# Another order of the attention step, with one weight piece per step

## The chip, the cores and the metric

The kernel runs on one core of a Trainium2 chip. The metric is the device time of one execution in microseconds. One core has five engines that run side by side and meet only at semaphores: TensorE (PE in the profile, its weight loads PEld), VectorE (DVE), ScalarE (ACT), GpSimd (POOL) and SyncE (SP), which here issues DMAs alone.

## The reference

32 samples are turned into rows of 256 numbers: 1 class row, 36 image patches and 77 text tokens, the text after four recurrent layers. On these 114 rows per sample follows one attention block and one mixture of experts. Cut to what the change touches:

```python
n = layernorm(h)
qk = silu(n @ wqk + bqk);  q = qk * gamma[0] + beta[0];  k = qk * gamma[1] + beta[1]
v = silu(n @ wv + bv)
attn = where(causal, laplacian(q @ k.T / S + bias), 0)
h = h + attn @ v
x = layernorm(h)
logits = x @ w_router.T            # 8 experts, the best 2 of each row, softmax over both
h = h + layernorm(sum of the two experts' outputs, weighted) * gain + bias
```

## The kernel before

The text layers run first, up to about 550 us of the span, then the attention stage, then 64 blocks of 128 sorted rows through the experts (from 715 us), and the final sums.

The attention stage works on 8 groups of 4 samples. Each engine has a function `attn_step(g)` (ACT line 958, POOL line 1182, PE line 1504, DVE line 1984) that is called for g = 0 to 10, unrolled. The order of the calls in it is the order of the engine's instructions, and engines take their instructions strictly in that order. In step g the attention of group g is computed, the attended sums of group g-1 are added, the normalized rows of group g-2 are turned and routed, and the rows of group g-3 get their places and are sent. In detail:

- ACT: `query_key_silu`, `query` and `key` make q and k of group g. `norm_rows(g+1)` and `rows_turned(g+1)` normalize the next group and copy its transposes from PSUM (banks 0 and 1). `gate_values(g, half)` makes the values, `score_gelu(g)` the gelu, with a load of the activation table on either side. `routed_norm(g)` (870) normalizes the rows for the router, `routed_turned` (882) copies their transposes (banks 6 and 0), and `weight(g)` (887) waits for DVE's `choose(g)`, which has the gap between the two best logits.
- PE: `query_key`, `values`, `scores`, `attended(g, half)` (1399), `turn_rows` (1374) and `turn_routed` (1411) for the transposes, `router` (1421: 16 products of 8 columns) and `ranks` (1431). `turn_rows(g+1, 0)` writes bank 0, so it waits until both parts of `routed_turned(g-2)` are done. `query_key(g)` needs both parts of `rows_turned(g)`.
- DVE: `scale_scores`, `invert` (1900, a reciprocal), `weigh`, `add_attended`, the statistics of both norms, `choose` (1934) and `count` (1946) for the best experts, `place_rows` (1965).
- POOL: the inverse roots of the norms, and `send_rows` (1166), 8 indirect DMAs for each group, 64 in all, that scatter the rows into `xrows` in DRAM. The first expert block is loaded when all have landed.
- SP: lines 667 to 671 load the gate and up weights in 8 pieces of 1 MB, two at a time: the next two are issued when the former two have landed (`ld_ffn`) and enough groups are added (`a_h2`). The first two have neither wait; they stand behind the loads of `h_all`.

Six of the pieces have to be split into an upper part (ACT, `upper_weights(k)`, line 826, waits for `ld_ffn` to show pieces 2*(k//2) and 2*(k//2)+1) and a lower part (DVE, `lower_weights(k)`, line 1869, waits for the upper one). Before, three are split in the tail of the attention stage (ACT in step 8, DVE in step 10) and three after it.

Of the kernel before, what the change touches and what calls it, by code (L numbers as in the profile page):

```python
# [22 lines left out]
GROUPS = BATCH // GB  # L23
# [145 lines left out]
def has(g):  # L169

    return not isinstance(g, int) or 0 <= g < GROUPS


def build(nc, patches, patches_tail, tokens, tok_w, tok_b, cls, pos_enc, tok_emb, pos_emb, w_in, w_b, w_c, w_out,
          small, ln_gb, wqk, wv, bv, rel_bias, w_gate, w_up, w_down, ffn_gb, consts, out):
    ctx = ExitStack()
    with ctx:
# [158 lines left out]
        assert at[0] <= 3 * FC * GT  # L336

        EMBEDDED = 5
        SPLIT_FIRST = 3
        BIAS_OPS = 3 * 3 + 11  # L340
        LAST_LAG = 3
        SENT_FIRST = 5
# [377 lines left out]
        def _(act):  # L720
# [105 lines left out]
            def upper_weights(k):  # L826
                act.wait_ge(ld_ffn, 32 * (k // 2 + 1))
                hi, _, raw = FFN_HALVES[k]
                act.activation(hi, raw, ACT.Copy).then_inc(w_upper, 1)

            def norm_rows(g):
                act.wait_ge(a_bias, g + 1)
                wait(act, a_tr, g * 2)
                for b in range(GB):
                    norm = act.activation(a_n[:, b, :], h_all[:, g * GB + b, :], ACT.Identity, bias=a_nb[:, b:b + 1],
                                          scale=a_rs[:, 0, b:b + 1])
                norm.then_inc(a_norm, 1)
# [6 lines left out]
            def query_key_silu(g):  # L844
                act.wait_ge(a_qkm, g + 1)
                wait(act, a_qkd, g)
                act.activation(a_qk, bank[2][:, 0:GS], ACT.Silu, bias=SML(W_QK)).then_inc(a_qks, 1)

            def query(g):
                act.wait_ge(a_qks, g + 1)  # L850
                wait(act, a_sm, g)
                act.activation(a_q, a_qk, ACT.Identity, bias=SML(W_QK + 3), scale=SML(W_QK + 1))

            def key(g):
                act.activation(a_k, a_qk, ACT.Identity, bias=SML(W_QK + 4), scale=SML(W_QK + 2)).then_inc(a_qkd, 1)

            def score_gelu(g):
                act.activation(warm[:, 0:1], minus_half[0:1, 0:1], ACT.Gelu)
                act.wait_ge(a_sa, g + 1)
                wait(act, a_om, g * 2)  # L860
                act.activation(a_w, a_arg, ACT.Gelu).then_inc(a_er, 1)
                act.activation(warm[:, 1:2], minus_half[0:1, 0:1], ACT.Silu)

            def gate_values(g, half):
                act.wait_ge(a_vm, g * 2 + (half + 1))
                wait(act, a_om, g * 2 - 1 + half)
                act.activation(a_v[:, 2 * half:2 * half + 2, :],
                               bank[3][0:SEQ, :].rearrange("p (k d) -> p k d", k=2), ACT.Silu).then_inc(a_vs, 1)

            def routed_norm(g):  # L870
                act.wait_ge(m_bias, g + 1)
                if g == 0:
                    for half in range(2):
                        act.wait_ge(seq_stored[2 + half], 16 * len(rows_out[half]) * GROUPS // 2)
                wait(act, m_tr, (g - ROW_SETS) * 2 + 2)
                wait(act, x_sent[g % ROW_SETS], g // ROW_SETS * (16 * 2 * GB))
                for b in range(GB):
                    norm = act.activation(a_x[g % ROW_SETS][:, b, 0:D], h_all[:, g * GB + b, :], ACT.Identity,
                                          bias=m_nb[:, b:b + 1], scale=m_rs[:, 0, b:b + 1])
                norm.then_inc(m_norm, 1)  # L880
# [77 lines left out]
            def attn_step(g):  # L958
                if has(g) and g:
                    query_key_silu(g)  # L960
                if has(g - 2):
                    routed_turned(g - 2, 0)
                    routed_turned(g - 2, 1)
                if has(g):
                    query(g)
                    key(g)
                if has(g + 1):
                    norm_rows(g + 1)
                if has(g - 2):
                    weight(g - 2)  # L970
                if has(g):
                    gate_values(g, 0)
                    score_gelu(g)
                if has(g + 1):
                    rows_turned(g + 1, 0)
                    rows_turned(g + 1, 1)
                if has(g):
                    gate_values(g, 1)
                if g - 1 == GROUPS - 1:
                    for k in range(SPLIT_FIRST):  # L980
                        upper_weights(k)
                if has(g - 1):
                    routed_norm(g - 1)

            for g in range(GROUPS + LAST_LAG):
                attn_step(g)


            for k in range(SPLIT_FIRST, len(FFN_HALVES)):
                upper_weights(k)  # L990

            def turn(j, k):
                act.wait_ge(f_tr, j + 1)
# [233 lines left out]
        def _(pe):  # L1227
# [276 lines left out]
            def attn_step(g):  # L1504
                if has(g) and g:
                    query_key(g)
                if has(g - 2):
                    turn_routed(g - 2, 0)
                    turn_routed(g - 2, 1)
                if has(g - 3):  # L1510
                    ranks(g - 3)
                if has(g):
                    values(g, 0)
                if has(g - 2):
                    router(g - 2)
                if has(g):
                    scores(g)
                if has(g - 1):
                    attended(g - 1, 0)
                    attended(g - 1, 1)  # L1520
                if has(g + 1):
                    turn_rows(g + 1, 0)
                    turn_rows(g + 1, 1)
                if has(g):
                    values(g, 1)
                if has(g + 1):
                    bias_scores(g + 1)

# [77 lines left out]
        def _(dve):  # L1606
# [377 lines left out]
            def attn_step(g):  # L1984
                if has(g - 3):
                    place_rows(g - 3)
                if has(g + 1) and g:
                    norm_bias(g + 1)
                if has(g + 2):
                    norm_ahead_stats(g + 2)  # L1990
                if g - 2 == GROUPS - 1:
                    for k in range(SPLIT_FIRST):
                        lower_weights(k)
                if has(g - 2):
                    choose(g - 2)
                if has(g):
                    scale_scores(g)
                if has(g - 1):
                    add_attended(g - 1, 0)
                    add_attended(g - 1, 1)  # L2000
                    routed_stats(g - 1)
                if has(g - 2):
                    count(g - 2)
                if has(g - 1):
                    routed_bias(g - 1)
                if has(g):
                    invert(g)
                    weigh(g)

            for g in range(GROUPS + LAST_LAG):  # L2010
                attn_step(g)
# [34 lines left out]
            dve.tensor_copy(expert_i[:, :], expert_f).then_inc(tbl_ready, 1)  # L2046
            c.done()
            dve.wait_ge(tbl_ready, 2)
            for k in range(SPLIT_FIRST, len(FFN_HALVES)):
                lower_weights(k)  # L2050


            def hidden(j, k):
# [151 lines left out]
```

## Time and profile before

| what | us |
|---|---|
| median of 3 runs | 1121.9 (1121.77, 1121.9, 1126.06) |
| profiled execution, its own time | 1125.7 |
| its span | 1123.9 |
| text layers, until about | 550 |
| attention stage, first gelu to last `slot_i` | 554.9 to 692.4 |
| last row sent to first expert product | 708.7 to 716.7 |
| PE busy | 975.9 (87%) |
| DVE, ACT, POOL busy | 758.9, 601.9, 577.5 |

The span goes from the first to the last instruction; the execution's own time has 1.8 us around it. The attention stage has eleven steps, of which eight bear the whole attention of a group.

### The profile page before, as it was taken

The numbers are of one execution on the slowest core, as the hardware profiler recorded it, in microseconds if no ns is written. First come the engines' busy times: TensorE is split into PE (matmuls) and PEld (weight loads), VectorE is DVE, ScalarE is ACT, GpSimd is POOL, SyncE is SP. The second block draws the span as 40 slices with busy tenths as digits, with TensorE's granted clock in tenths as the row PEclk, the third lists the DMA queues.
The fourth block names the chain that finished last, engine by engine and source line by source line (L and its number), as shares of the span: only waits on it lengthen the run. The fifth ranks groups of instructions, "written<-read, shape, count | busy, mean of one in ns | idle before, by whom it ended". The sixth has DMA issues, their size and how long they took to land.

```text
span 1123.9 us, 20592 instructions
## 1 busy us (share of the span) xinstructions
PE 975.9 (87%) x5838; PEld 846.4 (75%) x5839; DVE 758.9 (68%) x1966; ACT 601.9 (54%) x1343; POOL 577.5 (51%) x630
## 2 busy tenths in 40 slices
PE   5878999999999999999898962499999999999910
PEld 4668999999999999998666652377777777777710
DVE  1666999999999998998678767244444444444447
ACT  1466776877788777666697753123223223223223
POOL 4523765567667766777627767232222222222236
PEclk8998999999999999999999975699999999999965
DMA  9451001000100000012168236133233333333263
GB/s 278 130 151 57 1 1 66 1 2 1 67 1 2 1 25 2 10 58 57 36 212 260 61 76 224 52 47 50 47 47 49 49 47 47 47 50 48 43 162 118
DMA packets 54733, 75.49 MB, mean 67 GB/s; under 512 B 9348, under 2 KB 46978, under 8 KB 52612
## 3 DMA queue, kind: packets, MB, share of 16 engines
q1 hardware_dynamic: 32680, 49.24, 14.5%
q0 software_dynamic: 16640, 18.53, 10.1%
q10 hardware_dynamic: 5340, 6.83, 2.2%
q8 instruction: 36, 0.59, 0.2%
q14 instruction: 37, 0.30, 0.1%
HBM read 45.38 MB, written 29.14 MB: 66 GB/s over the span
## 4 chain that ended last, share of the span: by engine, by line
PE 68%; DVE 10%; POOL 7%; DMA 5%; issue 4%; ACT 3%; SPq 2%; POOLq 0%; ACTq 0%; DVEq 0%
PE bank L1264 16%; PE bank L1580 10%; PE bank L1329 7%; PE bank L1557 6%; PE bank L1566 5%; PE bank L1565 4%; PE bank L1324 3%; POOL xrows L1174 3%; PE bank L1560 3%; PE bank L1572 2%; DMA xtok<-in_tok_emb,tokens_s 2%; PE bank L1312 2%; SPq L541 1%; POOL xtok L1052 1%; DVE arena_b L1736 1%
## 5 line engine op out<-in xcount | busy, mean ns | idle before, releaser
L1203 POOL DMA_INDIRECT yrows<-arena_b,dest_i x64 | 99.2, 1550 | 268.2 <-ACT arena_b L1009 260.3
L1736 DVE SCALAR_TENSOR_TENSOR arena_b<-bank,sml,arena_b 128x304 f32<-128x304 f32 (+2 forms) x384 | 195.3, 522 | 20.7 <-ACT arena_b L778 17.9
L1264 PE MATMUL bank<-xt_hi,w_hi 128*128 128x308 f32 x512 | 159.9, 312 | 4.6 <-DVE arena_b L1736 3.2
L1264 PE MATMUL bank<-xt_hi,w_lo 128*128 128x308 f32 x512 | 157.3, 307 | 0.0
L1264 PE MATMUL bank<-xt_lo,w_hi 128*128 128x308 f32 x512 | 156.9, 306 | 0.0
L2057 DVE TENSOR_TENSOR arena_b<-bank,arena_b 128x512 f32<-128x512 f32 x64 | 44.3, 691 | 140.5 <-PE bank L1566 76.7
L1090 POOL TENSOR_TENSOR u_halves<-arena_b,u_halves 128x308 fp32r<-128x308 f32 x128 | 109.8, 865 | 29.8 <-ACT arena_b L790 29.7
L1084 POOL TENSOR_TENSOR y_lo<-arena_b,y_hi 128x308 fp32r<-128x308 f32 x128 | 107.9, 857 | 27.2 <-ACT y_hi L802 27.0
L1264 PEld LDWEIGHTS bank<-xt_hi,w_hi 128*128 128x128 f32 x512 | 98.0, 191 | 5.4 <-DVE arena_b L1736 3.5
L1580 PE MATMUL bank<-arena_b 128*128 x384 | 98.7, 393 | 1.2 <-DVE arena_b L2073 0.9
L1264 PEld LDWEIGHTS bank<-xt_hi,w_lo 128*128 128x128 f32 x512 | 98.0, 191 | 0.0
L1264 PEld LDWEIGHTS bank<-xt_lo,w_hi 128*128 128x128 f32 x512 | 97.8, 191 | 0.0
L1174 POOL DMA_INDIRECT xrows<-arena_b,slot_i x64 | 77.7, 1214 | 33.7 <-issue 16.9
L778 ACT ACTIVATE arena_b<-bank,sml 128x308 f32<-128x308 f32 x128 | 77.0, 602 | 17.4 <-PE bank L1264 12.0
L1002 ACT ACTIVATE arena_b<-bank 128x512 f32<-128x512 f32 x64 | 38.4, 599 | 85.5 <-PE bank L1560 85.5
L2073 DVE COPY arena_b<-bank 128x512 f32<-128x512 f32 x64 | 44.3, 691 | 56.6 <-PE bank L1572 56.6
L1329 PE MATMUL bank<-w_hi,y_hi 128*128 128x256 f32 (+1 forms) x320 | 82.1, 283 | 0.0
L1329 PE MATMUL bank<-w_lo,y_hi 128*128 128x256 f32 (+1 forms) x320 | 81.6, 282 | 0.0
L1744 DVE SCALAR_TENSOR_TENSOR bank<-arena_b,sml,bank 128x308 f32<-128x308 f32 x128 | 68.1, 534 | 19.5 <-PE bank L1313 19.3
L1009 ACT ACTIVATE arena_b<-bank,row_wt 128x256 f32<-128x256 f32 x64 | 30.4, 475 | 93.5 <-PE bank L1580 93.5
L1580 PEld LDWEIGHTS bank<-arena_b 128*128 128x128 f32 x384 | 67.8, 189 | 16.0 <-issue 5.9
L995 ACT ACTIVATE x_hi<-bank 128x256 fp32r<-128x256 f32 x64 | 24.6, 384 | 95.9 <-PE bank L1547 95.9
(212 smaller groups left out, 2650.3 us busy)
## 6 DMA issues: line engine op xcount, KB each, us to landing
arena_b<-xrows SPq DMA_DIRECT2D x64, 129.5 KB, 2.1
wg_raw<-in_w_gate SPq DMA_DIRECT2D x4, 1024.0 KB, 7.1
yrows<-arena_b SPq DMA_DIRECT2D x1, 3648.0 KB, 18.7
h_all<-seq SPq DMA_DIRECT2D x8, 448.0 KB
w_raw<-in_w_in SPq DMA_DIRECT2D x3, 1024.0 KB, 4.8
arena_b<-in_w_down SPq DMA_DIRECT2D x3, 1024.0 KB, 8.6
wu_raw<-in_w_up SPq DMA_DIRECT2D x2, 1024.0 KB, 7.3
wu_s<-in_w_up SPq DMA_DIRECT2D x2, 1024.0 KB, 9.4
```

Of the source, the lines that this page charges most:

```text
L778: act.activation(u[s % 2][:, c, :], x_bank(c)[:, 0:GT], ACT.Identity, bias=SML(W_CB + s // GROUPS * FC + c), scale=conv_w(s // GROUPS, c, ...
L1084: pool.tensor_tensor(y_half(y_lo, s, c), y_full[:, c, :], y_half(y_hi, s, c).bitcast(F32), ALU.subtract)\
L1090: pool.tensor_tensor(u_halves[s % 2][:, 1, c, :], u[s % 2][:, c, :], u_halves[s % 2][:, 0, c, :].bitcast(F32), ALU.subtract).then_inc(pool ...
L1174: pool.indirect_dma_start(xrows, bass.IndirectOffsetOnAxis(ap=to, axis=0), a_x[g % ROW_SETS][:, b, :], None).then_inc(x_sent[g % ROW_SETS] ...
L1203: pool.indirect_dma_start(yrows, bass.IndirectOffsetOnAxis(ap=dest_i[:, m:m + 1], axis=0), f_y[m % 2], None, compute_op=ALU.add).then_inc( ...
L1264: mm = pe.matmul(out_, in_half(w, layer, d, slice(c * P, (c + 1) * P)), x[:, d, cols], start=(k == 0), stop=(k == len(pairs) - 1))
L1329: return pe.matmul(out_tile(j), y[:, c, PAIR_AT[j]:PAIR_AT[j] + PAIR_ROWS[j]], out_half(w, s // GROUPS, c), start=False, stop=stop, skip_g ...
L1557: pe.matmul(bank[0][:, :], x_hi[:, k, d, :], w[:, d, cols], start=(d == 0 and w is wg_hi), stop=False)
L1566: pe.matmul(bank[1][:, :], x_raw[k], wu_s[:, cols], start=False, stop=True).then_inc(f_um, 1)
L1580: mm = pe.matmul(bank[4 + k][:, 0:D], f_ht[k][:, c, :], wd_s[c][:, bass.ds(e * D, D)], start=(c == 0), stop=(c == FC - 1))
L1736: dve.scalar_tensor_tensor(acc[:, :, back_:TXT], x[:, :, 0:TXT - back_], conv_w(s // GROUPS, c, tap), acc[:, :, back_:TXT], ALU.mult, ALU. ...
L1744: dve.scalar_tensor_tensor(y1, u[s % 2][:, c, :], SML(W_D + s // GROUPS * FC + c), y1, ALU.mult, ALU.add)\
```

## The change

ACT: `routed_norm` moves from the end of a step to its beginning and one step later (group g-2 in step g), `routed_turned` behind it into mid-step, `score_gelu` from mid-step to near the end; `weight` now stands ahead of `rows_turned`. PE: `turn_routed` moves from the head of the step behind the first half of `attended`, `turn_rows` ahead of `router`, and the halves of `attended` stand around `router` and `values(g, 1)`. DVE: `choose` and `count` stand together behind `invert`, between the two halves of `add_attended`. The split of the weights is spread: `upper_weights(0)` to `(5)` stand in ACT's steps 2 to 7, `lower_weights(0)` to `(5)` in DVE's steps 3 to 8. The programs of POOL and SP stay as they are.

```diff
--- before.py
+++ after.py
@@ -336,7 +336,7 @@
         assert at[0] <= 3 * FC * GT
 
         EMBEDDED = 5
-        SPLIT_FIRST = 3
+        SPLIT_FROM = 2
         BIAS_OPS = 3 * 3 + 11
         LAST_LAG = 3
         SENT_FIRST = 5
@@ -958,36 +958,32 @@
             def attn_step(g):
                 if has(g) and g:
                     query_key_silu(g)
+                if has(g):
+                    query(g)
+                    key(g)
+                if has(g - 2):
+                    routed_norm(g - 2)
+                if has(g + 1):
+                    norm_rows(g + 1)
+                if 0 <= g - SPLIT_FROM < len(FFN_HALVES):
+                    upper_weights(g - SPLIT_FROM)
                 if has(g - 2):
                     routed_turned(g - 2, 0)
                     routed_turned(g - 2, 1)
                 if has(g):
-                    query(g)
-                    key(g)
-                if has(g + 1):
-                    norm_rows(g + 1)
+                    gate_values(g, 0)
                 if has(g - 2):
                     weight(g - 2)
-                if has(g):
-                    gate_values(g, 0)
-                    score_gelu(g)
                 if has(g + 1):
                     rows_turned(g + 1, 0)
                     rows_turned(g + 1, 1)
                 if has(g):
+                    score_gelu(g)
                     gate_values(g, 1)
-                if g - 1 == GROUPS - 1:
-                    for k in range(SPLIT_FIRST):
-                        upper_weights(k)
-                if has(g - 1):
-                    routed_norm(g - 1)
 
             for g in range(GROUPS + LAST_LAG):
                 attn_step(g)
 
-
-            for k in range(SPLIT_FIRST, len(FFN_HALVES)):
-                upper_weights(k)
 
             def turn(j, k):
                 act.wait_ge(f_tr, j + 1)
@@ -1504,25 +1500,25 @@
             def attn_step(g):
                 if has(g) and g:
                     query_key(g)
-                if has(g - 2):
-                    turn_routed(g - 2, 0)
-                    turn_routed(g - 2, 1)
                 if has(g - 3):
                     ranks(g - 3)
                 if has(g):
                     values(g, 0)
+                    scores(g)
+                if has(g - 1):
+                    attended(g - 1, 0)
+                if has(g - 2):
+                    turn_routed(g - 2, 0)
+                    turn_routed(g - 2, 1)
+                if has(g + 1):
+                    turn_rows(g + 1, 0)
+                    turn_rows(g + 1, 1)
                 if has(g - 2):
                     router(g - 2)
                 if has(g):
-                    scores(g)
+                    values(g, 1)
                 if has(g - 1):
-                    attended(g - 1, 0)
                     attended(g - 1, 1)
-                if has(g + 1):
-                    turn_rows(g + 1, 0)
-                    turn_rows(g + 1, 1)
-                if has(g):
-                    values(g, 1)
                 if has(g + 1):
                     bias_scores(g + 1)
 
@@ -1988,24 +1984,24 @@
                     norm_bias(g + 1)
                 if has(g + 2):
                     norm_ahead_stats(g + 2)
-                if g - 2 == GROUPS - 1:
-                    for k in range(SPLIT_FIRST):
-                        lower_weights(k)
-                if has(g - 2):
-                    choose(g - 2)
+                if 0 <= g - 1 - SPLIT_FROM < len(FFN_HALVES):
+                    lower_weights(g - 1 - SPLIT_FROM)
                 if has(g):
                     scale_scores(g)
                 if has(g - 1):
                     add_attended(g - 1, 0)
+                if has(g):
+                    invert(g)
+                if has(g - 2):
+                    choose(g - 2)
+                    count(g - 2)
+                if has(g - 1):
                     add_attended(g - 1, 1)
                     routed_stats(g - 1)
-                if has(g - 2):
-                    count(g - 2)
+                if has(g):
+                    weigh(g)
                 if has(g - 1):
                     routed_bias(g - 1)
-                if has(g):
-                    invert(g)
-                    weigh(g)
 
             for g in range(GROUPS + LAST_LAG):
                 attn_step(g)
@@ -2046,8 +2042,6 @@
             dve.tensor_copy(expert_i[:, :], expert_f).then_inc(tbl_ready, 1)
             c.done()
             dve.wait_ge(tbl_ready, 2)
-            for k in range(SPLIT_FIRST, len(FFN_HALVES)):
-                lower_weights(k)
 
 
             def hidden(j, k):
```

## Rows read from the trace of the kernel before

**Rows 1.** Timeline of ACT, steps 3 and 7: start us, us, engine, line, what [idle before]
```profile
585.39 0.62 ACT L847 ACTIVATE arena_b<-bank,sml 128x456 f32<-128x456 f32 x1
586.18 0.99 ACT L885 ACTIVATE arena_a<-bank 128x456 f32<-128x456 f32 x2 [0.17 <-PE bank L1417]
587.06 0.77 ACT L852 ACTIVATE arena_b<-arena_b,sml 128x456 f32<-128x456 f32 x1
...
588.38 2.06 ACT L835 ACTIVATE arena_b<-h_all,a_nb,a_rs 114x256 f32<-114x256 f32 x4
591.98 0.21 ACT L890 ACTIVATE arena_b<-arena_b 114x4 f32<-114x4 f32 x1 [1.53 <-DVE arena_b L1944]
592.55 0.60 ACT L867 ACTIVATE arena_b<-bank 114x512 f32<-114x512 f32 x1 [0.36 <-PE bank L1407]
593.16 1.28 ACT L858 ACT_TABLE_LOAD   x1
...
596.56 0.96 ACT L842 ACTIVATE arena_b<-bank 128x456 f32<-128x456 f32 x2
...
598.78 2.08 ACT L878 ACTIVATE arena_b<-h_all,arena_a,arena_b 114x256 f32<-114x256 f32 x4 [0.77 <-DVE arena_a L1930]
...
646.63 0.62 ACT L847 ACTIVATE arena_b<-bank,sml 128x456 f32<-128x456 f32 x1
```

**Rows 2.** Timeline of POOL: first send, a send beside DVE's split, last send
```profile
588.87 1.24 POOL L1174 DMA_INDIRECT xrows<-arena_b,slot_i  x1 [6.06 <-DVE slot_i L1981]
...
681.95 2.27 POOL L1174 DMA_INDIRECT xrows<-arena_b,slot_i  x1 [2.39 <-DVE slot_i L1981]
...
708.65 1.11 POOL L1174 DMA_INDIRECT xrows<-arena_b,slot_i  x1 [0.30 <-issue]
```

**Rows 3.** Timeline of PE, end of the sends to the first expert block
```profile
715.40 0.66 PE L1547 MATMUL bank<-cst,arena_b 128*128 128x128 f32 x2 [22.32 <-DMA arena_b<-xrows]
```

**Rows 4.** Timeline of PE, step 3, at the full clock
```profile
587.21 1.98 PE L1395 MATMUL bank<-arena_a,arena_b 128*114 128x256 f32 x8
589.03 1.67 PE L1427 MATMUL bank<-sml,arena_a 128*114 128x8 f32 x16
...
591.42 1.89 PE L1407 MATMUL bank<-arena_b 114*114 114x256 f32 x8
593.15 0.94 PE L1380 MATMUL bank<-cst,arena_b 114*128 114x114 f32 x8
...
597.57 1.80 PE L1387 MATMUL bank<-arena_b,arena_a 128*128 128x456 f32 x4 [0.73 <-ACT arena_b L842]
```

**Rows 5.** Issues of line 671 on SP: duration ns min/median/max, first and last start us
```profile
L671 SPq DMA_DIRECT2D wg_raw<-in_w_gate x4: 327/398/433, 574.4 to 584.8; - x4
```

**Rows 6.** Waits on SP's queue, 540 to 720 us: us in total, times, longest
```profile
SPq L670 <- DMA wg_raw<-in_w_gate: 15.5, 2, 9.1
```

**Rows 7.** Timelines of ACT and DVE: three pieces of weights each
```profile
669.07 5.50 ACT L829 ACTIVATE wg_hi<-wg_raw 128x2048 fp32r<-128x2048 f32 x3
...
680.94 6.68 DVE L1872 TENSOR_TENSOR wg_lo<-wg_raw,wg_hi 128x2048 fp32r<-128x2048 f32 x3
```

**Rows 8.** Timeline of PE where the clock is low
```profile
616.13 1.00 PE L1417 MATMUL bank<-cst,arena_b 114*128 114x114 f32 x8 [1.39 <-ACT arena_b L878]
...
617.81 3.37 PE L1395 MATMUL bank<-arena_a,arena_b 128*114 128x256 f32 x8
...
660.90 1.78 PE L1417 MATMUL bank<-cst,arena_b 114*128 114x114 f32 x8 [4.02 <-ACT arena_b L878]
...
664.46 3.23 PE L1427 MATMUL bank<-sml,arena_a 128*114 128x8 f32 x16 [1.15 <-DVE slot_i L1981]
```

**Rows 9.** Stretches: us, busy us of PE, PEld, DVE, ACT, POOL, then PEclk
```profile
600.00:602.00 2.00, 1.10 (x12) 1.10 (x12) 1.90 (x2) 1.82 (x5) 1.40 (x2) 1.00 0.68 148
...
619.00:620.00 1.00, 1.00 (x4) 0.78 (x3) 1.00 (x5) 1.00 (x4) 0.59 (x1) 0.50 0.27 85
...
667.00:668.00 1.00, 1.00 (x5) 0.98 (x6) 0.24 (x2) 0.00 (x0) 0.79 (x1) 0.50 0.34 98
```

## The prediction

> **What bounds the kernel now.** I looked first at the chain of work that ended last, from 560 to 760 us, to see which engine carries the attention stage. It changes hands: ACT and PE in steps 0 to 2 and 5 to 8, POOL's indirect sends in steps 3 to 5 and from 681.95 us to the end. Then the timeline of each engine. ACT's step 3 goes from 585.39 to 600.76, and steps 3 to 6 take (646.63 - 585.39) / 4 = 15.3 us on average [rows 1]. In it ACT stands still in three places only: 1.53 us for the choice of the experts ahead of `weight`, 0.36 for `attended`, 0.77 for the bias ahead of `routed_norm`. The reader is to see how full the step is: nothing can be added to ACT without making it longer, unless a wait shrinks. POOL issues 64 sends from 588.87 to 708.65, of 1.11 us with 0.30 between them [rows 2]; 63 of these make 89 of the 120 us, and most of the rest are norms and waits, so POOL is the next bound, not far behind. The stage ends with POOL's last send, 6.75 us before the first transposes of the expert blocks at 715.40 [rows 2, 3]. The expert blocks themselves are not touched, nor are the text layers; all of the difference must come out between 555 and 715 us.
>
> **The early steps.** In steps 0 and 1 the gelu moves behind `rows_turned`, so `query_key` of the next group need not wait for two table loads. That saves some 3 us by the time of step 2, by my estimate. It is worth nothing, because of the next part.
>
> **The first weight piece.** ACT reaches `upper_weights(0)` in step 2, after q and k (0.62 + 1.32 = 1.94) and two norms of 2.0 each [rows 1], so some 6 us into the step. Step 2 begins at 571 at the latest (585.39 less a step of about 14), so that is 577 at the latest and 574 with the early gain. It waits there for both of the first pieces. SP issues these from 574.4 on, behind the loads of `h_all`, which nothing here moves; and the next two issues stood 9.1 us in the queue for their landing [rows 5, 6]. Two issues of 0.4 and 9.1 us put the landing at 584.3. ACT therefore stands still for 7 to 10 us, and behind it stand `routed_turned(0)`, `gate_values(2, 0)`, the gelu, and by them `turn_rows(3)`, the router and everything that PE has left in the step. From 584.3: the piece 1.83 (5.50 / 3) [rows 7], `routed_turned` 0.88 (586.18 to 587.06) [rows 1], so 587.0. PE has then had no product for some 13 us, and after 4.02 us without one its clock was at 0.50, where 8 transposes took 1.78, the router 3.23 and `values` 3.37 [rows 8, 9]. So: `turn_rows` 1.8, router 3.2, `values` 3.4, `attended` 1.9 (half of 1.89 at twice the time [rows 4]), the bias products about 0.8, `query_key` 1.7, which ends at about 600. Step 3 begins at 600 and not at 585.4: **+14.6 us**. At the full clock it would be 596, or +10.5.
>
> **The steps 3 to 6.** ACT's work in a step: q and k 1.94, two norms 4.0, a piece 1.83, `routed_turned` 0.88, two `gate_values` 1.0, `weight` 0.1, `rows_turned` 0.9, gelu with its tables 3.40 (593.16 to 596.56) [rows 1, 7]: 14.05 us. To this a new wait: `weight` stands ahead of `rows_turned`, and its chain starts only when `routed_turned` is done: `turn_rows` 0.9 (it needs bank 0 free), the router, the choice on DVE. From the router's start (589.03) to `weight` (591.98) is 2.95 us [rows 1, 4]. Of 3.85 us, `gate_values` covers 0.5, so ACT idles 3.35 us in each step where it idled 1.53. Before, `values`, q, k and `norm_rows` lay beside this chain; now nothing does. A step is **17.4 us** at the full clock, and 15.6 even without the piece. DVE (its piece 2.23 [rows 7], ahead of `scale_scores`) and POOL (8 sends, 11.3, and its norms) have room in 17.4; what is late next on DVE is `place_rows`, which waits out the routed norm's bias, but no step hangs on it. The other queue past which something moves is SP's: its third pair of pieces waits for the sums of group 1, which come at about 593 to 598 instead of 580; the pieces are needed two steps later.
>
> **The clock** decides between 17.4 and more. From `scores` to the router's end PE has in each step some 8 us in which it does 32 short transposes and products and nothing at all for about 3.2 us, between `turn_routed` and `turn_rows`. The rows have three gaps to compare: after 4.02 us the clock was 0.50, and stayed there through a router and two `attended`; in a step with a gap of 1.39 us followed by transposes it was 0.50 from 618 to 621; around a gap of 1.54 us that followed the dense `query_key` it stayed at 1.00 at 600 to 602 [rows 8, 9]. A gap of 3.2 with transposes on both sides is nearest to the first two. With the low clock (1.2 in place of 2.4 GHz) `turn_rows` costs 0.9 more and the router 1.6 more, 19.9 us by ACT. But then PE is later than ACT: 8.65 to the end of `routed_turned`, 1.8, 3.2, `values` 3.4, `attended` 0.9 to 1.9, the sum on DVE that frees bank 2 about 0.9, `query_key` 1.7: 20.6 to 21.6, and a little less if the clock is back during `values`. I take 20.8: **+5.5 us a step**, over four steps **+22**. The bounds are 17.4 (+8.4) and 21.6 (+25).
>
> The Trainium skill ("TensorE: Matmul & The Clock Gate", Part 1) says that an idle array falls to 1.2 GHz and only sustained activity lifts it, which speaks against this order. By that rule the forecast stands; by the gap of 1.54 us alone, which the clock survived, it would be 14 us lower.
>
> **The tail.** From step 7 (646.63) to 715.40 are 68.8 us [rows 1, 3]. The three lower pieces, 6.68 us [rows 7], no longer stand on DVE ahead of the last choice, nor do they and the later three lengthen sends (2.27 beside them, 1.24 without [rows 2, 7]). In their place one upper piece stands in step 7 and one lower in step 8, 4.1 us, about half hidden by waits of the routed norm. Between -6.7 and -2.6 I take **-5**. The clock in the tail was low already [rows 9].
>
> **The sum**: 14.6 + 22 - 5 = +31.6 us on the profiled execution's own 1125.7, so 1157.3. The profiled execution was 3.8 us above the median of the runs, so the median is forecast at 1153.5, and I say **1153**. From the bounds: 10.5 + 8.4 - 6.7 = +12 and 14.6 + 25 - 2.6 = +37; this case's own range is 1143 to 1160.
>
> **The rivals.**
> *The clock holds in steps 3 to 6.* The steps are 17.4 us: +14.6 + 8.4 - 7 (a little more, as step 7 is fast too) = +16, 1138. For it: 600 to 602 us. Against: the length of the gap, and what lies around it. Chance 0.24.
> *The first pieces don't stall ACT*, since they land sooner than in this trace or ACT comes later. Then step 3 starts near 586, and the steps cost +8 to +22, less 5: 1125 to 1140, say 1132. Nothing in the rows speaks for it but that the second pair, waiting 15.5 - 9.1 = 6.4 us, landed faster [rows 6]; 2.7 us sooner would still stall. Chance 0.05.
> *POOL sets the end and the order of the others is hidden* (the other side, not slower). Place: the 64 sends. They need 63 x 1.41 = 89 us and about 17 of norms and lengthened sends, 106, where 119.8 passed [rows 2]. If POOL never waited, its first send some 10 us later than 588.87 would still end the stage 3 to 4 us sooner: 1118. It decides from where ACT's step falls to 14.4 us, that is its wait for the choice to 0.35 us. The count of 3.35 says it doesn't. Chance 0.04.
> *The change does less than it says*: the new waits are as long as the old ones and only the tail gains. 1117 to 1125. Chance 0.02.
> The forecast has 0.65.
>
> **How the numbers follow.** The range must leave out at most 2 in 10. It takes in the forecast's case with its upper end, where the low clock also slows `values` and `scores` of the next step (three more us in each step, 1166), and the held clock with a few us below it: 1133 to 1167. About 0.5% (5.6 us) is what a measurement of this kernel can tell from no change. Slower by more: 0.65 + 0.24 + 0.04 of the stall's case = 0.93. Faster 0.03, same 0.04.
>
> **What would show it.** In the changed kernel's timeline of ACT: an idle time of 7 to 10 us ahead of the first upper piece, which starts at about 584.3; steps 3 to 6 of 20 to 21 us between the starts of `query_key_silu`; an idle time ahead of each `weight` of 3.4 us or, with the low clock, near 6, put down to the choice on DVE. On PE, gaps of about 3 us ahead of `turn_rows`, then a router near 3.2, and a granted clock of 0.50 there. No split of weights on DVE after the last choice; the last send at about 740. The forecast is wrong if the first upper piece starts before 580, if the steps are under 16 us, or if the clock stays at 1.00 from 600 to 680.

## The result, and the profile after

The changed kernel takes **1163.0 us** (median of 6 runs, 1157.4 to 1166.5) against 1123.9 for the kernel before in the same runs (6, 1121.4 to 1127.0): 1.0345 times as long, 95% interval 1.0312 to 1.0378, so 39 us slower. Forecast were 1153 and a range of 1133 to 1167. The profiled execution took 1164.9 (span 1163.0), which is 39.2 above that of the kernel before; the sums below are made on these two.

The top of the page of the changed kernel: busy time and share of each engine, then the granted clock in 40 slices.

```profile
PE 996.2 (86%) x5838; PEld 861.6 (74%) x5839; DVE 758.6 (65%) x1966; ACT 601.5 (52%) x1343; POOL 583.5 (50%) x630
...
PEclk8899999999999999999977885599999999999965
```

The counts are those of before (5838, 1966, 1343, 630), and so is the busy time of DVE and ACT within half a microsecond: the same work in another order. PE is busy 20.3 us longer with the same products, because the clock is at 7 to 8 tenths in slices 21 to 24, where it was at 9 before. The other 19 us are idle time of PE.

The timeline of ACT in the changed kernel, steps 2 and 3 with the start of step 4 (start us, us, engine, line, what, then in brackets the idle time ahead and what ended it), for [rows 1]. Line 829 is `upper_weights`, 885 `routed_turned`, 890 `weight`, 842 `rows_turned`:

```profile
572.14 0.62 ACT L847 ACTIVATE arena_b<-bank,sml 128x456 f32<-128x456 f32 x1
...
582.94 1.91 ACT L829 ACTIVATE wg_hi<-wg_raw 128x2048 fp32r<-128x2048 f32 x1 [4.79 <-DMA wg_raw<-in_w_gate]
...
599.91 0.62 ACT L847 ACTIVATE arena_b<-bank,sml 128x456 f32<-128x456 f32 x1
...
605.83 1.89 ACT L829 ACTIVATE wg_hi<-wg_raw 128x2048 fp32r<-128x2048 f32 x1
607.62 0.96 ACT L885 ACTIVATE arena_a<-bank 128x456 f32<-128x456 f32 x2
608.48 0.58 ACT L867 ACTIVATE arena_b<-bank 114x512 f32<-114x512 f32 x1
613.48 0.21 ACT L890 ACTIVATE arena_b<-arena_b 114x4 f32<-114x4 f32 x1 [4.41 <-DVE arena_b L1940]
616.68 0.99 ACT L842 ACTIVATE arena_b<-bank 128x456 f32<-128x456 f32 x2 [2.99 <-PE bank L1391]
617.69 1.28 ACT L858 ACT_TABLE_LOAD   x1
...
621.56 0.61 ACT L847 ACTIVATE arena_b<-bank,sml 128x456 f32<-128x456 f32 x1
```

Line 847 is `query_key_silu`, the start of a step. Steps 1 to 7 start at 559.75, 572.14, 599.91, 621.56, 644.31, 665.99 and 688.79, and PE's first transposes of the expert blocks stand at 754.45. In the kernel before they started at 559.75, 571.23, 585.39, 600.76, 615.99, 632.14 and 646.63, and the transposes at 715.40. So the 39.05 us come in three places:

| | before | after | difference | forecast |
|---|---|---|---|---|
| start of step 3 | 585.39 | 599.91 | +14.5 | +14.6 |
| steps 3 to 6 | 61.24 | 88.88 | +27.6 | +22 |
| step 7 to the expert blocks | 68.77 | 65.66 | -3.1 | -5 |

PE in the changed kernel, its transposes of step 2 and then step 3, for [rows 4, 8]. A row without brackets had no idle time ahead of it:

```profile
585.87 1.75 PE L1376 MATMUL bank<-cst,arena_b 114*128 114x114 f32 x8 [8.63 <-ACT arena_a L885]
...
608.73 0.97 PE L1376 MATMUL bank<-cst,arena_b 114*128 114x114 f32 x8 [3.72 <-ACT arena_a L885]
609.54 2.66 PE L1423 MATMUL bank<-sml,arena_a 128*114 128x8 f32 x16
...
612.83 3.76 PE L1391 MATMUL bank<-arena_a,arena_b 128*114 128x256 f32 x8
...
618.52 1.77 PE L1383 MATMUL bank<-arena_b,arena_a 128*128 128x456 f32 x4 [0.46 <-DVE h_all L1909]
```

Line 1376 is `turn_rows`, 1423 the router, 1391 `values`, 1383 `query_key`. The gap of 3.72 us stands ahead of `turn_rows`, and soon behind it the clock falls: the router takes 2.66 and not 1.67, `values` 3.76 and not 1.98. The stretches of the changed kernel give the clock (us, then busy us of PE, PEld, DVE, ACT and POOL with their counts, PEclk, DMA share, GB/s), for [rows 9]:

```profile
599.90:621.60 21.70, 16.38 (x76) 12.44 (x76) 14.43 (x55) 14.20 (x26) 10.46 (x10) 0.84 0.39 136
621.60:644.30 22.70, 18.06 (x76) 13.93 (x76) 14.71 (x55) 14.09 (x25) 13.29 (x13) 0.77 0.48 147
...
611.00:616.00 5.00, 5.00 (x16) 3.77 (x16) 2.56 (x23) 0.21 (x1) 1.40 (x3) 0.50 0.10 30
```

From 611 to 616 the clock is at 0.50, which is 1.2 GHz in place of 2.4, and PE is busy for all of it. ACT works 14.2 us of 21.7 in a step, as counted (14.05). The rest is the two waits in ACT's rows above, 4.41 and 2.99 us, and the second of them, ahead of `rows_turned` (line 842), stood in no sum.

POOL sends from 602.82 to 747.08 and in each of these steps stands idle for 4.6 to 8.9 us at a time, so it bounds nothing in steps 3 to 6. [rows 2] has its last send 6.75 us ahead of the expert blocks; here it starts at 747.08, 7.37 us ahead of them (the prediction had it at about 740).

### The profile page after: what moved, and what is told of

The parts are those of the page before. It is cut to its first block and busy times, and to the rows that moved or that the text cites. A ratio compares the mean times of both kernels' runs of the same rounds, so it can differ in the third digit from the quotient of the medians.

```text
span 1163.0 us, 20591 instructions
## 1 busy us (share of the span) xinstructions
PE 996.2 (86%) x5838; PEld 861.6 (74%) x5839; DVE 758.6 (65%) x1966; ACT 601.5 (52%) x1343; POOL 583.5 (50%) x630
## 5 line engine op out<-in xcount | busy, mean ns | idle before, releaser
L1170 POOL DMA_INDIRECT xrows<-arena_b,slot_i x64 | 82.2, 1284 | 20.8 <-issue 16.6
L1576 PEld LDWEIGHTS bank<-arena_b 128*128 128x128 f32 x384 | 67.8, 189 | 15.8 <-issue 6.0
```

Source lines behind the costliest of these rows:

```text
L1170: pool.indirect_dma_start(xrows, bass.IndirectOffsetOnAxis(ap=to, axis=0), a_x[g % ROW_SETS][:, b, :], None).then_inc(x_sent[g % ROW_SETS] ...
L1576: mm = pe.matmul(bank[4 + k][:, 0:D], f_ht[k][:, c, :], wd_s[c][:, bass.ds(e * D, D)], start=(c == 0), stop=(c == FC - 1))
```

## The experiments

All are compared with the kernel before, which took 1124.6 to 1125.3 us in these runs. A step is always from one `query_key_silu` to the next.

Two accounts of the later steps are tested. **The choice** is the prediction's: the first piece stalls ACT, the chain through the choice of the experts lengthens each step, the low clock more so, and `rows_turned` is held by the `weight` ahead of it. **The buffer** came from the fence above. `rows_turned(g)` waits for `a_vm` at 2g, which is the end of `values(g - 1, 1)`, since both share the buffer `a_nt`. The change put the router, which has to wait for `routed_turned`, directly ahead of `values(g, 1)`, and moved `rows_turned` ahead of the gelu. ACT's chain is then turned rows, router, `values`, `rows_turned`, gelu, `query_key_silu`, whatever `weight` does.

The expectations have letters. In the first five runs A is the prediction's three causes (stall, longer chain, low clock), B the pieces' own work and C the waits without the clock. In the three runs from the second buffer on, A is the buffer and D the choice. In the last two A is a gain where a piece fills a wait, and E no gain.

### The first piece one step later

```diff
-        SPLIT_FROM = 2
+        SPLIT_FROM = 3
```

> The changed kernel with every weight piece one step later (upper ones in steps 3 to 8, lower ones in steps 4 to 9). Theory A, three causes that add up (the wait for the first pieces in step 2, the longer chain of the new order, the low clock in it): the wait of 4.8 us before the first piece and the cold restart behind it go, step 3 begins near 589 and not at 599.9, steps 3 to 6 keep their 22.2 us, and the time is some 9 us less, about 1154. Rival B, the pieces' own work on ACT and DVE is what costs: there is as much of it as before, so 1163 within 2 us.

Measured: 1155.5 us, 1.0254 (1.0223 to 1.0286), near the 1154 expected. ACT's step 2 goes from 570.68 to 591.73, 21.05 us, against 27.77 in the changed kernel and 14.16 before. So of the 13.6 us that step 2 grew, the piece and its restart are 6.7, and 6.9 would be there without: a step of the new order at the low clock with no piece in it (the granted clock of that step is 0.76). The steps 3 to 6 stay long, at 21.7 on average. The pieces' own work (rival B, 1163) is not what costs the 39 us.

### The order alone, and the pieces alone

The order with the pieces where they were (three at the end of step 8, three behind the stage); and the kernel before with one piece a step:

```diff
# the order alone, ACT (DVE in the same way)
-                if 0 <= g - SPLIT_FROM < len(FFN_HALVES):
-                    upper_weights(g - SPLIT_FROM)
...
+                if g - 1 == GROUPS - 1:
+                    for k in range(SPLIT_FIRST):
+                        upper_weights(k)
...
# the pieces alone, ACT (DVE in the same way)
                     norm_rows(g + 1)
+                if 0 <= g - SPLIT_FROM < len(FFN_HALVES):
+                    upper_weights(g - SPLIT_FROM)
                 if has(g - 2):
                     weight(g - 2)
...
```

> The changed order of the attention step alone, with the weight pieces in the tail as in the kernel before. Theory A: step 3 begins near 588; the gap on PE ahead of turn_rows shrinks to about 2 us; if the clock still falls the steps are near 20.4 us and the time is 1146 to 1150, if it holds they are near 16.5 and the time is about 1132. Rival B: without the pieces in the steps the time is back at 1124 to 1128.

> The order of the kernel before with one weight piece per step from step 2. Theory A: the wait for the first pieces costs some 8 us in step 2, the steps after it stay between 15.0 and 15.8 us since a piece of 1.8 us takes the place of the 1.5 us wait for the choice, and the tail is some 5 us shorter: 1126 to 1131. Rival B: most of the 39 us comes with the pieces, over 1150.

Measured: the order alone 1144.6 us, 1.0159 (1.0120 to 1.0197); the pieces alone 1133.6, 1.0075 (1.0053 to 1.0098). Neither 1132 nor the other branch of the first expectation came quite true, and the pieces cost a little more than expected. From 1124.9 the parts cost 19.7 and 8.8 us, 28.5 together; the change costs 39. Some 10 us arise only when both are there. In the profiles they stand in steps 3 to 6: there the order alone costs 8.9 us, the pieces alone 4.0 and the change 27.6. Order alone, ACT in step 4:

```profile
619.51 0.99 ACT L885 ACTIVATE arena_a<-bank 128x456 f32<-128x456 f32 x2 [0.29 <-PE bank L1417]
620.38 0.61 ACT L867 ACTIVATE arena_b<-bank 114x512 f32<-114x512 f32 x1
624.40 0.21 ACT L890 ACTIVATE arena_b<-arena_b 114x4 f32<-114x4 f32 x1 [3.41 <-DVE arena_b L1944]
625.55 0.99 ACT L842 ACTIVATE arena_b<-bank 128x456 f32<-128x456 f32 x2 [0.93 <-PE bank L1395]
```

And PE in that step, with the stretch of it:

```profile
618.92 0.94 PE L1417 MATMUL bank<-cst,arena_b 114*128 114x114 f32 x8
620.64 0.97 PE L1380 MATMUL bank<-cst,arena_b 114*128 114x114 f32 x8 [0.78 <-ACT arena_a L885]
...
613.20:630.40 17.20, 14.69 (x76) 11.46 (x76) 12.84 (x54) 12.47 (x24) 11.82 (x13) 0.90 0.66 187
```

Here the wait for the choice is 3.41 us, which the prediction had at 3.35, and `rows_turned` waits for `values` even so (0.93). Steps 4 to 6 are 17.2. Without the piece ACT reaches `routed_turned` sooner, so PE's gap ahead of `turn_rows` is 0.78 and not 3.72, and the router behind it runs at the full clock. Most of the 10 us should come from this: the piece stands ahead of `routed_turned`, and so in PE's gap, and the next experiment prices the low clock. But the order alone isn't free of the low clock either. Its step 2 takes 21.0 us at 0.76, with a gap of 1.92, and its step 3, with the same gap, 18.5.

In the pieces alone, ACT waits 8.10 us for the first piece in step 2, which takes 23.7 in place of 14.2. Its steps 3 to 5 are 16.7 to 16.8 each, where I had 15.8 or less. ACT waits 1.6 us for the bias of the routed norm, where it waited 0.77 in step 3 before; DVE's piece of 2.26 us stands ahead of that bias, but no run parts it from the rest. By step 7 both losses stand at 13.5 us, and the tail gives 3.5 of them back.

### The gap filled

To part the clock from the chain: products of constants into an unread part of bank 7, in the gap ahead of `turn_rows`. Twelve of them, then eight, which is about what the gap holds. The wait keeps them off bank 7 until the slots of group g-3 have been read. Nothing is left out of the computation.

```diff
+                if has(g - 2) and has(g + 1):
+                    wait(pe, m_slot, g - 2)
+                    for k in range(FILLERS):
+                        pe.matmul(bank[7][:, 256:512], ident, cst[:, 0:256], start=True, stop=True)
                 if has(g + 1):
                     turn_rows(g + 1, 0)
```

> The changed kernel with 12 products of 256 columns into an unread part of bank 7 between turn_routed and turn_rows in each full step, some 2.9 us of the 3.7 us in which PE stands still there. Theory A, the low clock costs 4 us of each step: the granted clock stays at 1.00 in steps 3 to 6, the router takes about 1.6 us and not 2.7 to 3.1, steps of 18 to 18.5 us, and the time is some 16 us less, about 1147. Rival C, the clock only follows from the waits and ACT sets the step: the steps stay over 21 us, 1160 to 1168.

> The changed kernel with 8 filler products in place of 12. The 12 took 5.4 us of PE and put turn_rows off by 1.5 us, though the clock stayed at 1.00. Theory A (the clock costs 3.8 us a step): 3.6 us of products end before routed_turned does, the clock still stays at 1.00, the steps fall from 19.9 to 18.4 us, 1148 to 1152. Rival C (the products only help by their place, 19.9 us is the chain at the full clock): steps stay at 19.9, or return to 22 as the clock falls, 1157 to 1163.

Measured: twelve 1157.0 us, 1.0281 (1.0251 to 1.0312), missed by 10; eight 1150.7, 1.0242 (1.0218 to 1.0267), as expected. PE in step 3 with twelve, with eight, each with a stretch of its steps:

```profile
602.33 5.36 PE L1517 MATMUL bank<-cst 128*128 128x256 f32 x24
607.52 0.95 PE L1377 MATMUL bank<-cst,arena_b 114*128 114x114 f32 x8
608.31 1.67 PE L1424 MATMUL bank<-sml,arena_a 128*114 128x8 f32 x16
...
597.40:617.30 19.90, 18.14 (x100) 14.57 (x100) 14.43 (x55) 14.17 (x26) 10.06 (x10) 1.00 0.40 138
```

```profile
602.47 3.63 PE L1517 MATMUL bank<-cst 128*128 128x256 f32 x16
606.36 0.97 PE L1377 MATMUL bank<-cst,arena_b 114*128 114x114 f32 x8 [0.26 <-ACT arena_a L886]
...
597.50:616.10 18.60, 16.60 (x92) 12.96 (x92) 14.43 (x55) 14.16 (x25) 10.22 (x10) 1.00 0.45 157
616.10:635.90 19.80, 17.98 (x92) 14.29 (x92) 14.76 (x55) 14.23 (x26) 14.01 (x13) 0.91 0.57 164
```

Twelve products take 5.36 us (each is two instructions in the trace, so x24); the gap is 3.72, and they put `turn_rows` off. The clock is 1.00 in each of steps 3 to 6 and a step takes 19.9. With eight (3.63 us) it takes **18.6** in the two steps at 1.00 (3 and 6) and 19.7 in the two at 0.91. The steps of the changed kernel take 22.2 on average. So the low clock costs 22.2 - 18.6 = 3.6 us a step, some 14 over four. The other 3.3 of the 6.9 us by which a step grew are the chain and the piece.

### A second buffer for the turned rows

The test of the buffer. Groups 2, 4 and 6 get their turned rows in a part of `wu_hi` that is still free, so `rows_turned` waits only for the `values` of two groups before. (PE's `query_key` and `values` read through the same `turned_rows(g)`, which the diff doesn't show.)

```diff
-                wait(act, a_vm, g * 2)
-                act.activation(a_nt[:, d, :], bank[d][:, 0:GS], ACT.Copy).then_inc(a_trc, 1)
+                wait(act, a_vm, max(g - 1, min(g, 1)) * 2)
+                act.activation(turned_rows(g)[:, d, :], bank[d][:, 0:GS], ACT.Copy).then_inc(a_trc, 1)
...
```

> The changed kernel with a second buffer for the turned rows (groups 2, 4 and 6), so that rows_turned no longer waits until values(g, 1) has read the first. Theory A (this wait is what the forecast left out): the 3 us of idle time ahead of rows_turned go in steps 1 to 6, ACT then waits for attended(g-1, 1) ahead of the gelu, and the steps come to the 20.8 us of the forecast, some 1.4 us shorter each, 1156 to 1158. Rival D (the wait for the choice ahead of weight is what makes the step): nothing changes, 1162 to 1165.

Measured: 1157.4 us, 1.0305 (1.0280 to 1.0329), as expected. This interval and that of the change (1.0312 to 1.0378) overlap a little, so it is the profile that decides. ACT in step 3, up to step 4:

```profile
613.20 0.21 ACT L894 ACTIVATE arena_b<-arena_b 114x4 f32<-114x4 f32 x1 [5.61 <-DVE arena_b L1944]
613.32 0.97 ACT L846 ACTIVATE wu_hi<-bank 128x456 f32<-128x456 f32 x2
614.30 1.28 ACT L862 ACT_TABLE_LOAD   x1
615.60 0.20 ACT L862 ACTIVATE warm<-minus_half 1x1 f32<-1x1 f32 x1
617.13 0.58 ACT L865 ACTIVATE arena_b<-arena_b 114x456 f32<-114x456 f32 x1 [1.32 <-PE bank L1407]
...
619.71 0.64 ACT L851 ACTIVATE arena_b<-bank,sml 128x456 f32<-128x456 f32 x1
```

`rows_turned` (line 846) follows `weight` at once, and the wait of 2.99 is gone; 1.32 of it comes back ahead of the gelu, for `attended`. Steps 3 to 6 take 82.6 us in place of 88.9, 20.65 each on average. This is the step that the prediction had costed, and it had it at 20.8.

### The weight later, and the values first

If `rows_turned` hangs on `values`, moving `weight` behind the gelu gives nothing by itself (by the account of the choice it would gain, as the step is then free of it); with `values(g, 1)` also ahead of the router the chain gets shorter.

```diff
# both, ACT
-                if has(g - 2):
-                    weight(g - 2)
                 if has(g + 1):
                     rows_turned(g + 1, 0)
                     rows_turned(g + 1, 1)
                 if has(g):
                     score_gelu(g)
+                if has(g - 2):
+                    weight(g - 2)
# the second alone, PE
-                if has(g - 2):
-                    router(g - 2)
                 if has(g):
                     values(g, 1)
+                if has(g - 2):
+                    router(g - 2)
```

> The changed kernel with ACT's weight(g-2) behind score_gelu. Theory A: the 4.4 to 5.5 us of idle time ahead of weight only move to rows_turned, which waits for values(g, 1) anyway; steps stay at 22.2 us, 1161 to 1165. Rival D (the choice ahead of rows_turned holds ACT up, as the forecast counted it): the steps get over 1 us shorter, 1158 or less.

> As the run with weight behind score_gelu, and on PE values(g, 1) ahead of router(g-2). Theory A: ACT's chain loses the router's 2.7 to 3.1 us, but PE's own sum does not change and query_key ends 1.4 us before ACT takes it; so the steps get about 1.4 us shorter, 1156 to 1158. Rival D: as the run before, no more and no less.

Measured: 1160.4 us, 1.0336 (1.0303 to 1.0369), and 1161.2 us, 1.0337 (1.0316 to 1.0358). Neither ratio can be told from that of the change. In the first the two waits have become one. ACT's rows for it in steps 3 and 4, with PE's router of step 4 between them, and in the second run the rows for it and for the next step:

```profile
614.87 0.99 ACT L842 ACTIVATE arena_b<-bank 128x456 f32<-128x456 f32 x2 [8.70 <-PE bank L1392]
...
629.47 1.68 PE L1424 MATMUL bank<-sml,arena_a 128*114 128x8 f32 x16
...
635.25 0.99 ACT L842 ACTIVATE arena_b<-bank 128x456 f32<-128x456 f32 x2 [6.25 <-PE bank L1392]
```

```profile
631.13 0.99 ACT L842 ACTIVATE arena_b<-bank 128x456 f32<-128x456 f32 x2 [4.69 <-PE bank L1392]
...
638.27 0.64 ACT L847 ACTIVATE arena_b<-bank,sml 128x456 f32<-128x456 f32 x1 [2.01 <-PE bank L1384]
```

8.70 us for `values` alone is what 5.51 and 3.00 were together in step 4 of the changed kernel, with `weight` between them: the router takes 3.12 us in both steps. There the choice didn't hold the step, it only named itself first. But the steps did not all stay at 22.2. Steps 3 and 6 take 22.8 and 23.0, steps 4 and 5 only 20.4 and 20.3. In those two the router runs at the full clock (1.68), in the others at the low one (3.12), so the gain is seen only where the clock differs; whether the move of `weight` brought that about is not shown.

With `values` ahead, the wait is 4.69 in step 4 and about 3.06 in the other three, and the step 20.3 on average. But now `query_key` is late: PE waits 2.22 us ahead of it for DVE's sum. DVE works on `choose` and `count` without a pause from the end of the router to that sum (611.90 to 614.62 in step 3), so here the choice does hold the step, by way of PE. In steps 5 and 6 `query_key` also runs at the low clock (3.38 us against 1.77). The tail is 2.0 us longer than in the changed kernel (67.6). The steps gave what the account of the buffer says; the total, which I had put at 1156 to 1158, didn't follow. Four steps at 20.3 are 7.5 us shorter; 2.0 go back in the tail and 1.4 in a longer step 2 (29.2 us), which leaves 4.1. Of these the medians show less than 2, within their uncertainty; that rest is open.

### Pieces where the engines stand still

The order of before is kept, and pieces go where ACT and DVE have idle time late in the stage; then also `ranks(g - 3)` ahead of `turn_routed(g - 2)` on PE, so that the slots of the sends come sooner.

```diff
+        UPPER_AT = {5: (0,), 6: (1,), 7: (2, 3)}
+        LOWER_AT = {6: (0,), 7: (1,), 8: (2,)}
...
# the second alone, PE
+                if has(g - 3):
+                    ranks(g - 3)
                 if has(g - 2):
                     turn_routed(g - 2, 0)
                     turn_routed(g - 2, 1)
-                if has(g - 3):
-                    ranks(g - 3)
```

Upper pieces 4 and 5 follow in step 8, lower ones 3 and 4 at the end of DVE's step 8 and 5 behind the tables.

> The order of the kernel before, with the weight pieces where its engines stand still: upper ones in ACT's steps 5 to 8 (1, 1, 2, 2), lower ones in DVE's steps 6, 7 and 8 (1, 1, 3) and one after the block tables. Theory A (pieces cost nothing where they fill a wait, and the 6.7 us ahead of the last choice go): steps up to 0.4 us longer in steps 5 and 6, the last 16 sends are no longer slowed by three pieces ahead of the choice, 2 to 5 us less than the kernel before. Rival E (POOL's sends and their slowing beside DVE's pieces make up for it wherever the pieces are): within 1 us of the kernel before.

> The same with ranks(g-3) ahead of turn_routed(g-2) on PE. The last but one group's slots no longer wait for the last group's norm and transposes (about 4.6 us of DVE's idle time at 675 to 680), so POOL goes on without its wait of 2.4 us: another 2 us less, 4 to 7 in all. If the last group's own chain sets the end instead: no difference to the run before.

Measured in 12 runs each: 1122.7 us, 0.9985 (0.9965 to 1.0004), which can't be told from the kernel before, and 1122.6, 0.9966 (0.9947 to 0.9985), which can: **0.3% faster** (0.15% to 0.5%). The two can't be told from each other, so the "another 2 us" expected of the second is not shown, and both lie at or under the low end of what was expected. From the start of step 2 to the expert blocks are 144.2 us before, 142.2 with the spread and 140.6 with both; but the steps 0 and 1 of the last took 26.2 us and not 24.8, with the same program in them, so the profiles don't part the two either. POOL in the last, at the sends of group 6, against the wait of 2.39 in [rows 2]:

```profile
676.44 3.25 POOL L1174 DMA_INDIRECT xrows<-arena_b,slot_i  x1 [0.23 <-issue]
680.00 1.82 POOL L1174 DMA_INDIRECT xrows<-arena_b,slot_i  x1 [0.30 <-issue]
682.12 1.12 POOL L1174 DMA_INDIRECT xrows<-arena_b,slot_i  x1 [0.30 <-DVE slot_i L1981]
```

The wait is gone, but two pieces on DVE have lengthened two sends by 2.1 and 0.7 us, which takes part of the gain.

## Why the prediction was right, and where it was not

The direction, the three places and, in the main, the mechanism held; the forecast of 31.6 us was 7.6 short on the profiled execution. The median is 10 above the 1153 that was said: the other 2 are the step from the profiled execution to the median, which was taken as 3.8 us from three runs and is 1.9 here. The sum's own upper bound of +37 gives 1159, under the measured 1163; the range held by the 8 us more that it had for `values` and `scores` of the next step slowed by the low clock. At the head of the changed kernel's steps these took 1.98 and 0.96 us, as at the full clock, and what came instead was the wait for a buffer. That is partly luck, and so is the size of the first place.

- **The early steps.** "Some 3 us" were to be gained by step 2 and then hidden. They were never there: step 2 starts at 572.14, 0.9 us later than before, and ACT waited 3.00 and 2.62 us for `values` (line 1391) ahead of `rows_turned` in steps 0 and 1. It is the same semaphore as below.
- **The first piece: +14.6, measured +14.5.** ACT's wait was 4.79 us and not 7 to 10, as it came later and the piece landed at 582.9, not 584.3. PE's gap was 8.63 and not 13; the clock fell all the same (`turn_rows` 1.75, the router 3.12, `values` 3.76 where 1.8, 3.2 and 3.4 were written). The total is right but its name is half wrong: 0.9 are already there at the start of step 2, and the run with the piece one step later shows that 6.7 of the rest are the stall with its restart and 6.9 the new order at the low clock, which falls in step 2 without a stall too. Two errors cancel in the sum: the piece started 1.4 us earlier than written, and from it to step 3 passed 17.0 us, not 15.7.
- **Steps 3 to 6: +22, measured +27.6.** This is the term that was mis-sized, and it went above its bound of +25: a step of 17.4 us at the full clock, and 20.8 at the low. The filled gap puts the first at 18.6, and the profile the second at 22.2. What was left out is `rows_turned`'s wait for the end of `values(g, 1)`. The prediction gave ACT one new wait, the choice; the order alone shows it at 3.41 us where 3.35 was written, and 0.93 for `values` behind it. At the low clock it is 4.4 to 5.6 and then 3.0. With the second buffer the step is 20.65, the forecast one, and 6.3 us of these four steps come back. That covers the 5.6 by which the term was short; the other 2 of the 7.6 are the tail.
- **The clock.** The rival that it holds (0.24) fell. Each step has its gap of 3.72 us between short transposes, where the prediction had 3.2, and a stretch at 0.50. Filling the gap brings 1.00 back and takes 3.6 us off the step; 3.4 was the difference written between 17.4 and 20.8. The gap of 1.54 us that the clock survived was the wrong row to argue from. The Trainium skill ("TensorE: Matmul & The Clock Gate", Part 1) says that an idle array falls to 1.2 GHz. The trace agrees: 0.50 from 611 to 616, behind a gap of 3.72 us.
- **The tail: -5, measured -3.1**, within its bounds of -6.7 and -2.6, and argued, not tested. DVE's pieces are gone from ahead of the last choice, but two of the sends beside pieces of steps 7 and 8 still stretch.
- **POOL as the bound** (0.04) and **no stall** (0.05) fell: POOL stood idle for up to 8.9 us at a time, and ACT did wait for the transfer. That the change does less than it says (0.02) fell as well.
- **The bounds.** +12 and +37 on the median of 1121.9 give 1134 to 1159; the "1143 to 1160" written behind them does not follow for its lower end.

## What to carry to other kernels

When an operation is moved on one engine, look up every semaphore that its end releases, those that free a buffer (write after read) too, and follow each to the engine that waits for it; the profile of before shows no idle time for a wait that is long satisfied. Of two waits in a row on an engine the first one hides the second: `weight` was named in the profile, and moving it gave nothing in the steps with the same clock. And a piece of work that "fits" on an engine costs twice if PE stands idle behind it and comes back at the low clock: here 1.4 us a step with the clock held (18.6 with the gap filled, 17.2 in the order alone), and 3.6 more by the clock.

## What the runs showed that I had not expected

**A send waits out DVE's piece, to the end.** The rows of DVE and POOL in step 4 of the changed kernel:

```profile
624.96 2.26 DVE L1868 TENSOR_TENSOR wg_lo<-wg_raw,wg_hi 128x2048 fp32r<-128x2048 f32 x1
```

```profile
625.00 3.21 POOL L1170 DMA_INDIRECT xrows<-arena_b,slot_i  x1 [0.30 <-issue]
628.51 1.12 POOL L1170 DMA_INDIRECT xrows<-arena_b,slot_i  x1 [0.30 <-issue]
```

DVE's piece ends at 627.22 and the send at 628.21, 0.99 us later. For each of the six sends that began beside a piece (at 604.36, 625.00, 648.31, 667.96, 691.32 and 708.03) the end is 0.99 to 1.01 us behind the piece's, whatever part of it was still ahead, so they took 2.49 to 3.21 us where an undisturbed one takes 1.12. Here a piece thus costs POOL up to 2.1 us, and only one send pays; [rows 2, 7] show the same (681.95 and 2.27, against the first third of 6.68). The Trainium skill ("SBUF — State Buffer", "Who interferes with whom") says that an instruction of DVE with two inputs in SBUF contends with one of GpSimd that reads SBUF. The trace agrees with that if these sends are such instructions, which the six ends suggest; no run here changes the form of DVE's piece to test it.

**The clock also fell behind smaller gaps.** With a gap of 3.72 us ahead of `turn_rows` it fell in every step of the changed kernel. In the order alone the gap is 1.92 us in steps 2 and 3. In step 2 the router behind it took 3.12 us; in step 3 it took 1.68, and the clock fell only while PE was busy with `values` (3.67 us, 0.50 from 604.6 to 608). With 0.78 (order alone, step 4) the router took 1.67 us, but the stretch still had 0.90: `values` and `scores` at the head of that step, behind a gap of 1.28, took 2.71 and 1.75 us, against 1.98 and 0.96 where the clock was full. So in these traces the length of the gap alone doesn't tell which products run slow. Eight products of constants, 3.63 us, held 1.00 in two steps of four and 0.91 in the others; twelve held it in all.
